# Rope of two heads in one 128-partition instruction, K and Q placed by 128 KB transfers, units in a new order

## What is computed

```python
q, k, v = (einsum('bse,fe->bsf', x, w).reshape(B, S, 16, 64) for w in (w_q, w_k, w_v))
q, k = rope(q), rope(k)        # pairs (a, b) -> (a*cos - b*sin, a*sin + b*cos)
att = einsum('bqhd,bkhd->bhqk', q, k) / 8
att = softmax(where(causal, att, -inf))
y = einsum('bhqk,bkhd->bqhd', att, v)
t = t + einsum('bsf,ef->bse', y, w_o)
```

## Time and profile before

| | |
|---|---|
| median of three runs | 4394.03 us |
| the profiled execution: its own time | 4394.59 us |
| its span, first to last instruction | 4392.8 us |
| attention loop, first to last row of maxima | 1107.3 to 3567.8 us |
| busy share of the span | TensorE 78%, VectorE 67%, ScalarE 52%, GpSimd 47% |
| mean granted clock of TensorE | 0.874 |

### The profile page before, as it was taken

How to read it: one execution, slowest core, us unless ns; L and a number is a source line. 1 busy time by engine, 2 the same in 40 slices (tenths; PEclk the granted TensorE clock), 3 DMA queues, 4 the chain that set the end, 5 groups by cost and what they waited for, 6 DMA issues and landing times. The chain is left out here.

```text
span 4392.8 us, 64538 instructions
## 1 busy us (share of the span) xinstructions
PE 3431.4 (78%) x19824; PEld 2647.5 (60%) x19824; DVE 2940.9 (67%) x4313; ACT 2272.4 (52%) x3207; POOL 2067.2 (47%) x1576
## 2 busy tenths in 40 slices
PE   6233333333999999999999999999999958999998
PEld 1122222222666666676666667666666737898988
DVE  2344444444788888888888888888888865655646
ACT  0000000001677777777777777777777744554545
POOL 0577777775555555555555555555555540000000
PEclk8555555555999999999999999999999978999999
DMA  4533333333122222212122221222222132333333
GB/s 90 142 94 94 94 94 94 94 94 93 53 57 57 57 57 62 57 43 62 53 57 62 57 57 48 57 57 57 57 62 57 43 83 99 122 120 105 132 104 110
DMA packets 171257, 339.66 MB, mean 77 GB/s; under 512 B 61496, under 2 KB 78776, under 8 KB 170936
## 3 DMA queue, kind: packets, MB, share of 16 engines
q1 hardware_dynamic: 143544, 263.18, 20.6%
q0 software_dynamic: 27648, 75.53, 5.9%
HBM read 246.09 MB, written 24.38 MB: 62 GB/s over the span
## 5 line engine op out<-in xcount | busy, mean ns | idle before, releaser
L1033 DVE TENSOR_TENSOR attention_probs_l<-attention_probs,attention_probs_h 128x896 fp32r<-128x896 f32 (+4 forms) x768 | 843.0, 1098 | 65.0 <-ACT attention_probs_h L942 64.8
L938 ACT ACTIVATE attention_probs<-attention_pss 128x896 f32<-128x896 f32 (+4 forms) x768 | 623.7, 812 | 476.0 <-PE attention_pss L804 469.2
L991 DVE TENSOR_REDUCE attention_mx<-attention_pss 128x1 f32<-128x256 f32 (+7 forms) x1032 | 728.5, 746 | 197.2 <-PE attention_pss L820 196.3
L415 POOL DMA_INDIRECT deform_gat<-table,deform_idx x576 | 671.3, 1166 | 208.0 <-issue 170.6
L942 ACT ACTIVATE attention_probs_h<-attention_pss 128x896 fp32r<-128x896 f32 (+4 forms) x768 | 620.4, 808 | 0.0
L1043 POOL TENSOR_TENSOR attention_qk<-attention_tA,attention_tB 128x512 f32<-128x512 f32 x260 | 417.7, 1607 | 368.6 <-DVE attention_tB L1001 336.8
L817 PE MATMUL attention_pss<-attention_KA,attention_QA 128*128 128x512 f32 (+2 forms) x1548 | 480.9, 400 | 102.1 <-DMA attention_QA<-attention_QA 86.4
L1484 DVE SCALAR_TENSOR_TENSOR spectral_eo<-spectral_psE,spectral_sig,spectral_eo 64x512 fp32r<-64x512 f32 x512 | 383.9, 750 | 263.8 <-ACT spectral_eo L1463 259.2
L1075 POOL TENSOR_TENSOR kept_T<-kept_T,attention_scaled 128x512 f32 x129 | 206.2, 1598 | 713.3 <-DVE attention_scaled L980 673.6
L801 PE MATMUL attention_pss<-attention_QA,attention_KA 128*128 128x512 f32 (+4 forms) x1536 | 496.6, 377 | 20.6 <-ACT attention_probs_h L942 12.7
L1387 PE MATMUL spectral_psE<-spectral_tz,spectral_up 128*128 128x256 f32 (+2 forms) x3072 | 507.5, 324 | 4.4 <-DVE spectral_eo L1484 4.4
(11 more groups left out here) (174 smaller groups left out, 5656.8 us busy)
## 6 DMA issues: line engine op xcount, KB each, us to landing
spectral_tz<-phis SPq DMA_DIRECT2D x128, 320.5 KB, 4.6
spectral_tz<-phis SPq DMA_DIRECT2D x128, 320.0 KB, 4.2
attention_xb<-xn SPq DMA_DIRECT2D x67, 512.0 KB, 4.7
attention_wt<-wsplit SPq DMA_DIRECT2D x67, 512.0 KB, 5.4
attention_KB<-attention_KA SPq DMA_DIRECT2D x130, 256.0 KB, 3.4
attention_QA<-attention_QA SPq DMA_DIRECT2D x130, 256.0 KB, 3.5
table<-offsets_pixT SPq DMA_DIRECT2D x32, 288.0 KB
deform_gat<-table,deform_idx POOLq DMA_INDIRECT x576
```

What stands on the lines that cost most here:

```text
L415: pool.indirect_dma_start(gat[:, r, k, :, :].rearrange("p q c -> p (q c)"), None, d.table.rearrange("r q c -> r (q c)"), bass.IndirectOffs ...
L938: act.activation(probs[:, j % 2, 0:width], pss[:, slot, lead:lead + width], ACT.Exp, scale=float(E) ** -0.5)
L991: ins = dve.tensor_reduce(mx[:, nh % 2, i:i + 1], pss[:, slot, first:first + (i + 1) * P], AX.X, ALU.max)
L1033: dve.tensor_tensor(probs_l[:, cols], probs[:, j % 2, 0:widths(j)], probs_h[:, cols].bitcast(F32), ALU.subtract).then_inc(s_lo, 1)
```

## The change

The upper parts of both heads go in one ScalarE instruction of 128 partitions into a new tile `nat_h`, the lower parts in one GpSimd instruction into `nat_l`. From there SyncE's DMAs set every place in KA, KB, QA and QB: for each of the four units of a pair four transfers of 128 KB of the upper parts and two of the lower parts, 24 for a pair where there were four of 256 KB. SyncE's order is, for each unit: wait for the upper part, four transfers, wait for the lower part, two transfers. TensorE's waits count the landed transfers. The steps and units get a new order, and with them the places of `upper`, of the value products and of the token loads.

```diff
-STEPS = [(0,), (2,), (3,), (1,), (4, 5), (7, 6)]
+STEPS = [(0,), (7, 6), (1,), (3,), (2,), (4, 5)]
...
-    0: [[("rope", 0)], [("rope", 1), ("max", 5)], [("max", 7), ("rope", 2)], [("rope", 3), ("max", 4, 1), ("max", 0, 6)],
-        [("max", 3, 2)], [("out",), ("row",)]],
-    1: [[("max", 1, 5)], [("max", 7), ("max", 4, 2)], [("max", 3, 0)], [("max", 6)], [("out",), ("row",)], []],
+    0: [[("max", 0, 6), ("rope", 0), ("max", 5, 1), ("rope", 1)], [("rope", 2)], [("max", 3, 2)], [("rope", 3), ("max", 4)],
+        [("max", 7)], [("out",), ("row",)]],
+    1: [[("max", 4, 2)], [("max", 3, 1), ("max", 7)], [], [("max", 5, 0)], [("max", 6)], [("out",), ("row",)]],
...
-UPPER_AT = {1: 0, 2: 1, 3: 2, 4: 3}
+UPPER_AT = {0: 0, 2: 1, 3: 2, 4: 3}
...
-PV_AT = {(0, "end"): -2, (1, "end"): -1, (3, "before"): 0, (4, "before"): 1, (5, "after"): 2, (5, "end"): 3}
+KQ_COPIES = 16 * (2 * 6 + 2 * 4)
+PV_AT = {(0, "before"): -2, (1, "after"): -1, (2, "end"): 0, (4, "before"): 1, (4, "after"): 2, (5, "end"): 3}
...
+        nat_h = sb("nat_h", [P, 4, HB], F32R)
+        nat_l = sb("nat_l", [P, 4, HB], F32R)
...
-                def copy(pp, w, done):
-                    sp.wait_ge(s_H, done)
+                def copy(pp, r, done):
+                    w, c = divmod(r, 2)
+                    cols = slice(c * HB, (c + 1) * HB)
+                    sp.wait_ge(s_H, done + r + 3)
                     for n in range(2):
                         rows, others = slice(E * n, E * n + E), slice(E * (1 - n), E * (1 - n) + E)
-                        src = (KA, QA)[w][rows, 2 * pp + n, :]
-                        dst = KB[rows, 2 * pp + n, :] if w == 0 else QA[others, 2 * pp + n, :]
-                        sp.dma_start(dst.bitcast(F32), src.bitcast(F32)).then_inc(s_dup, 16)
+                        for dst in ((KA[rows, 2 * pp + n, cols], KB[rows, 2 * pp + n, cols]),
+                                    (QA[rows, 2 * pp + n, cols], QA[others, 2 * pp + n, cols]))[w]:
+                            sp.dma_start(dst.bitcast(F32), nat_h[rows, r, :].bitcast(F32)).then_inc(s_dup, 16)
+                    sp.wait_ge(s_low, done + r + 1)
+                    for n in range(2):
+                        rows, others = slice(E * n, E * n + E), slice(E * (1 - n), E * (1 - n) + E)
+                        if w == 0:
+                            sp.dma_start(KA[others, 2 * pp + n, cols].bitcast(F32),
+                                         nat_l[rows, r, :].bitcast(F32)).then_inc(s_dup, 16)
+                        else:
+                            sp.dma_start(QB[rows, 2 * pp + n, cols].bitcast(F32),
+                                         nat_l[rows, r, :].bitcast(F32)).then_inc(s_ql, 16)
...
-                            for w in range(2):
-                                copy(pp, w, 8 * it + (4 * (2 - pp) + 2 * w + 4))
+                            for r in range(4):
+                                copy(pp, r, 8 * it + 4 * (2 - pp))
...
-                            pe.wait_ge(s_L, 4 * (2 * it + h // 2) + 4)
+                            pe.wait_ge(s_dup, KQ_COPIES * (2 * it + h // 2) + KQ_COPIES)
+                            pe.wait_ge(s_ql, 64 * (2 * it + h // 2) + 64)
...
-                            pe.wait_ge(s_dup, 64 * (2 * it + (h + 1) // 2) + 64)
-                            pe.wait_ge(s_L, 4 * (2 * it + (h + 1) // 2) + 2)
+                            pe.wait_ge(s_dup, KQ_COPIES * (2 * it + (h + 1) // 2) + KQ_COPIES)
...
                     act.wait_ge(s_sum, R + r + 3)
-                    act.activation(dst[0:E, 2 * pp, cols], qk[0:E, r % 2, :], ACT.Copy)
-                    act.activation(dst[E:P, 2 * pp + 1, cols], qk[E:P, r % 2, :], ACT.Copy).then_inc(s_H, 1)
+                    act.activation(nat_h[:, r, :], qk[:, r % 2, :], ACT.Copy).then_inc(s_H, 1)
...
                     pool.wait_ge(s_sum, R + min(r + 2, 4) + 2)
-                    for n in range(2):
-                        rows, others = slice(E * n, E * n + E), slice(E * (1 - n), E * (1 - n) + E)
-                        slot = 2 * pp + n
-                        dst, up = (KA[others, slot, cols], KA) if w == 0 else (QB[rows, slot, cols], QA)
-                        pool.tensor_tensor(dst, qk[rows, r % 2, :], up[rows, slot, cols].bitcast(F32),
-                                           ALU.subtract).then_inc(s_low, 1)
-                        pool.wait_ge(s_low, 2 * R + 2 * r + n + 1)
-                    pool.sem_inc(s_L, 1)
+                    pool.tensor_tensor(nat_l[:, r, :], qk[:, r % 2, :], nat_h[:, r, :].bitcast(F32),
+                                       ALU.subtract).then_inc(s_low, 1)
+                    pool.wait_ge(s_low, R + r + 1)
```

More of the change, by code:

```diff
@@ L548, with half_steps @@
 FIRST_MAX = [[u for units in UNITS[h] for u in units if u[0] == "max"][0] for h in range(2)]
+def half_steps(half):
+    steps = [j for j, tiles in enumerate(STEPS) if any(t // 4 == half for t in tiles)]
+    return steps[0], steps[-1]
+HALF_STEPS = [half_steps(half) for half in range(2)]
 BODY_HEADS = 4
-UPPER_AT = {1: 0, 2: 1, 3: 2, 4: 3}
+UPPER_AT = {0: 0, 2: 1, 3: 2, 4: 3}
 SLOTS = 3
 PV_LAG = 2
-PV_AT = {(0, "end"): -2, (1, "end"): -1, (3, "before"): 0, (4, "before"): 1, (5, "after"): 2, (5, "end"): 3}
+KQ_COPIES = 16 * (2 * 6 + 2 * 4)
+PV_AT = {(0, "before"): -2, (1, "after"): -1, (2, "end"): 0, (4, "before"): 1, (4, "after"): 2, (5, "end"): 3}
 LEAVE_AT = 1
@@ L667, in attention_stage @@
         s_dup = sem("dup")
-        s_L = sem("L")
         s_low = sem("low")
+        s_ql = sem("ql")
         s_rec = sem("rec")
@@ L757, in _ @@
                 load(1, 0, 1)
-                for w in range(2):
-                    copy(0, w, 2 * w + 4)
+                for r in range(4):
+                    copy(0, r, 0)
                 sp.wait_ge(s_full, 4)
@@ L774, in _ @@
                     for half in range(2):
-                        sp.wait_ge(s_pv, BODY_HEADS * NS * CB * b + (BODY_HEADS * NS * CB + NS - 2 + 2 * half))
+                        sp.wait_ge(s_pv, BODY_HEADS * NS * CB * b + (BODY_HEADS * NS * CB + HALF_STEPS[half][1] + 1))
                         tokens(half, (b + 1) % B)
@@ L778, in _ @@
                 sp.wait_ge(s_in[1], 32 * NIT + 32)
-                sp.wait_ge(s_dup, 64 * (2 * NIT + 1))
+                sp.wait_ge(s_dup, KQ_COPIES * (2 * NIT + 1))
+                sp.wait_ge(s_ql, 64 * (2 * NIT + 1))
                 for half in range(2):
@@ L860, in pv @@
                         pe.wait_ge(s_y, BODY_HEADS * it + h + 1)
-                    if h == 0 and STEPS[j][0] in (0, 4):
-                        pe.wait_ge(s_xt[STEPS[j][0] // 4], 16 * b + 16)
+                    for half in range(2):
+                        if h == 0 and j == HALF_STEPS[half][0]:
+                            pe.wait_ge(s_xt[half], 16 * b + 16)
                     for kt_ in STEPS[j]:
@@ L947, in unit, with upper @@
                         act.activation(QB[row:row + 2, nh, :], pss[0:2, slot, :], ACT.Copy, scale=-1.0).then_inc(s_act, 1)
-                def upper(r, R, pp):
-                    w, c = divmod(r, 2)
-                    dst, cols = (KA, QA)[w], slice(c * HB, (c + 1) * HB)
+                def upper(r, R):
                     act.wait_ge(s_sum, R + r + 3)
-                    act.activation(dst[0:E, 2 * pp, cols], qk[0:E, r % 2, :], ACT.Copy)
-                    act.activation(dst[E:P, 2 * pp + 1, cols], qk[E:P, r % 2, :], ACT.Copy).then_inc(s_H, 1)
+                    act.activation(nat_h[:, r, :], qk[:, r % 2, :], ACT.Copy).then_inc(s_H, 1)
                 for n, (h, _, u) in enumerate(AHEAD):
@@ L959, in _ @@
                         for r in (2 * (n - 4), 2 * (n - 4) + 1):
-                            upper(r, 0, 0)
+                            upper(r, 0)
                     unit(h, u, n % SLOTS, n, -1)
@@ L968, in _ @@
                         if (n + 1 == N_BODY or ORDER[n + 1][2][0] == "S") and h % 2 == 0 and j in UPPER_AT:
-                            upper(UPPER_AT[j], 8 * it + (4 if h == 0 else 8), 1 - h // 2)
+                            upper(UPPER_AT[j], 8 * it + (4 if h == 0 else 8))
                 leave(NIT, -1)
@@ L1043, in add, with lower, pair @@
                     pool.tensor_tensor(qk[:, r % 2, :], tA[:, r % 2, :], tB[:, r % 2, :], ALU.add).then_inc(s_sum, 1)
-                def lower(r, R, pp):
-                    w, c = divmod(r, 2)
-                    cols = slice(c * HB, (c + 1) * HB)
+                def lower(r, R):
                     pool.wait_ge(s_H, R + r + 3)
                     pool.wait_ge(s_sum, R + min(r + 2, 4) + 2)
-                    for n in range(2):
-                        rows, others = slice(E * n, E * n + E), slice(E * (1 - n), E * (1 - n) + E)
-                        slot = 2 * pp + n
-                        dst, up = (KA[others, slot, cols], KA) if w == 0 else (QB[rows, slot, cols], QA)
-                        pool.tensor_tensor(dst, qk[rows, r % 2, :], up[rows, slot, cols].bitcast(F32),
```

(14 more changed lines are left out.)

## The result

The changed kernel takes 4536.06 us (median of four runs, 4534.97 to 4540.88) against 4394.14 for the kernel before in the same set of runs: a ratio of 1.0327, 95% interval 1.0309 to 1.0345. The forecast was 4600. The profiled execution took 4536.3 us, with a span of 4534.1.

The account below looks back on a forecast made before the run. Each pair was bound by an even half ending with the rope, add, upper part, DMA chain, and an odd half TensorE fills. 4394.6 + 96 (chain) + 113 (clock) = 4604, stated as 4600 us; 8-in-10 range 4372 to 4690.

Parts of the forecast that it names:

- The chain's start: Attention pair: first upper part ready at 6.5 us, lower 0 ends at 10.9, SyncE's 18 issues start at 10.95.
- Issues: SyncE's queue: 18 transfers between lower 0 and the odd head's first maximum, 0.64 us each, bounds 0.47 and 0.64.
- Landing: The pair's last awaited transfer lands 2.6 us after issue, at 24.7; TensorE goes on at 24.8, against 23.3 before.
- Even half without a wait: TensorE's work up to the odd head's first maximum, without DMA wait: 21.3 us in the new order, 21.9 before.
- One pair for all 64: Attention loop taken as periodic, so one timed pair of heads stands for all 64.
- Chain term: Late DMA chain before the odd head's first maximum: 1.5 us a pair, 64 x 1.5 = 96 us.
- Clock term: TensorE's clock falls behind the 3.5 us wait in 8 of 10 pairs, 2.2 us each: 113 us, bounds 0 to 218.
- Priced at nothing: Shorter upper and lower instructions save 2.5 us (ScalarE) and 5.2 us (GpSimd) a pair, counted as no gain in time.
- clock holds: Rival: SyncE's queue is late but TensorE's clock does not fall; 4490 us, chance 0.17.
- Issue does not queue: Rival: SyncE's issue time overlaps transfers, so the even half ends at 21.3, not 23.3; 4266 us, chance 0.13.
- issues cost 0.47: Rival: SyncE's issues take 0.47 us; 4375 us, or 4435 with occasional clock falls; chance 0.17.
- later still: Rival: transfers hold the DMA engines 0.8 us each, chain ends 2.7 us later; 4770 us, chance 0.05.

Follow-up runs that it names:

- eight or four fills: Changed kernel plus eight or four unused 512-column matmuls ahead of TensorE's wait at the odd head's first maximum: 4436.9 us with eight, 4453.2 us with four.
- tiny issues: Changed kernel with Q's lower-part transfers issued last, plus four unused 4 KB transfers in SyncE's chain: 4665.1 us, ratio 1.0623.
- new order, old moves: Changed kernel's new order of steps and units, with the old upper and lower instructions and four 256 KB copies: 4598.8 us, ratio 1.0470.
- lower Q last: Changed kernel, but SyncE issues the four transfers of Q's lower parts behind everything else, 16 issues in the chain, not 18: 4365.5 us.

## Why the prediction was right, step by step

- **The chain's start.** Foretold: first upper part 6.5, first lower part's issue 10.95. Measured 6.52 (2055.85) and 10.83 (2060.16). The exclusion of GpSimd and VectorE held: `lower` 1.60 and the add 2.21 us long beside VectorE's subtractions, 1.29 alone.
- **Issues.** 18 at 0.64 from there, last start at 22.1. Measured: the four of the last unit start at 2069.08 and end at 2071.54, so the last one starts near 2070.9, 21.6. The bound of 0.47 was rightly left to a rival; it is the time of an issue behind a wait (0.47 at 2055.85), not of one behind another.
- **Landing.** 2.6 taken, 2.3 measured; the maximum starts at 24.0 instead of 24.8.
- **Even half without a wait.** Placed by hand at 21.3; TensorE got there at 21.46 (2070.75, and 0.04 for that matmul). So the wait in the prediction's measure is 2.55, not 3.5 (2.36 of idle time in the row).
- **One pair for all 64.** The prediction took the pair to be 37.86 us (23.30 + 14.56) beside a mean of 38.4 from the same rows and left the 0.6 unexplained. It is the table load: it comes in every second pair, whose first odd maximum starts at 24.4 instead of 23.3. In the new order, without half clock (eight or four fills), the two kinds of pair have 24.0 and 25.3, so the load costs nearly the same in both orders, and the sum lost little by leaving it out.
- **Chain term.** 96 us foretold, 43 measured (53 within the loop). This is the mis-sized term: 1.5 us a pair was the difference of two numbers near 24, and 0.5 in the queue and 0.3 in the landing made it 0.7 (24.0 against 23.30).
- **Clock term.** 113 us foretold (2.2 a fall, 51 falls), 99 measured (92 within the loop; 65 stretches with 246 us at half clock, up to 123 us of work if all of it was full). The 47 falls behind the wait that I had named are near the 51, though the wait is 1 us shorter; that the total comes so near is partly luck, since 18 more falls stand behind a slot wait that I had not priced. The Trainium skill (TensorE: Matmul & The Clock Gate, HAM oscillation) tells of a kernel in which the clock falls at every DMA wait (of some 3 to 5 us) between two bursts of matmuls. Here it falls at 47 of 64 such waits, which are shorter (2.34 us); at the 3.64 us of the tiny issues it falls at all 64.
- **Engines.** GpSimd down by 330 foretold, 291 measured (its adds took 1706 ns in the mean over the run, 1607 before, and the additions to `kept_T` 1865, 1598 before); ScalarE 160 foretold, 187 measured.
- **"Priced at nothing".** In the old order the short instructions gain nothing (4405.9), but the new order can't do without them: with the long ones it took 4598.8.

Both terms were too large, by 53 and 14 us, so no error hid another: 4600 was said and 4536 came. Of the rivals, "clock holds" is what the kernel with eight fills shows (4436.9, with 43 us for the chain instead of 96). "Issue does not queue" and "issues cost 0.47" fell with the 0.64 us from start to start, "later still" with the landing after 2.3 us.

## What to carry to other kernels

Count the DMA issues in front of a wait, not their bytes: one queue issues one 64-partition transfer in 0.64 us here, and splitting four copies into 24 puts 15 us of issues in a pair of 38. Order the queue by who waits first; moving four transfers that nobody needed yet behind the rest turned a loss of 142 us into a gain of 29. Before giving issues to a second queue, look at the DMA share of that stretch: at 0.93 there was little left to gain. A wait of TensorE that grows past what the kernel had should be priced with the clock, which here cost more than the wait itself. And a pair that is shown in a timeline should be held against the mean over the loop: here every second pair holds a table load of 1.28 us.

## What had not been expected

- How often the clock falls at the wait before the first odd maximum goes steeply with that wait. Over the loops of all kernels but "new order, old moves" (where a longer wait stands just before it), none of 245 waits under 1.2 us has a fall within 2 us of its end, 7 of 132 from 1.2 to 1.6 us have one, 72 of 118 from 1.6 to 2.4 us, and all 78 of 2.4 us and more. All these kernels do much the same work around the wait, so this is no rule for others.
- A transfer of 4 KB and one of 128 KB cost SyncE the same 0.60 us and the distance of 0.64, and land 1.8 and 2.3 us after issue.
- With a second engine issuing, SyncE's transfers of the same size land at 3.6 us (ScalarE, at 12 + 4 issues in the chain) instead of 2.3, in a stretch with a DMA share of 1.04. Whether fewer bytes would bring the 2.3 back was not tried.
- The clock fell 18 times behind the slot wait of 1.62 us in the kernel after; the kernel with lower Q last has that same wait as often (31 times) and only 7 falls behind it. So it isn't the one wait alone; what of the work around it decides stays open. The kernel before, whose longest waits in the steady loop are 1.24 us for the DMA and 0.83 for the slot, has no fall there.
